# Transposes of the normalised block ahead of the attention output, the fold of the keys between the halves of the up-projection, and the gelu table load ahead of a copy

## The reference

```
x = x + xattn(layernorm(x), ctx)     # scores over 257 keys, 4 heads, top 32 kept, softmax, mean over heads,
                                     # @V; film; S4D convolution along 32 tokens; film; + residual;
                                     # h = gelu(layernorm(xt) @ W1 + b1) @ W2 + b2 (hidden 1024); layernorm
x = x + attn(layernorm(x))           # q, k, v; softmax(q k^T / 4) v, transposed and reshaped, @ wo^T
x = x + ffn(layernorm(x))            # 8 experts of hidden 128, top-2 gates (cosine + linear scores),
                                     # out = sum_e gate_e * (gelu(x @ w1_e + b1_e) @ w2_e + b2_e)
```

## Time and profile before

| | us |
|---|---|
| median of the runs | 654.56 |
| profiled execution | 650.08 |
| its span, first to last instruction | 648.1 |
| TensorE busy | 563.0 (87%) |
| VectorE busy | 519.7 (80%) |
| ScalarE busy | 304.0 (47%) |
| GpSimd busy | 270.8 (42%) |

### The profile page before, as it was taken

How to read it: one execution, slowest core, us unless ns; L and a number is a source line. 1 busy time by engine, 2 the same in 40 slices (tenths; PEclk the granted TensorE clock), 3 DMA queues, 4 the chain that set the end, 5 groups by cost and what they waited for, 6 DMA issues and landing times.

```text
span 648.1 us, 12648 instructions
## 1 busy us (share of the span) xinstructions
PE 563.0 (87%) x4314; PEld 420.1 (65%) x4314; DVE 519.7 (80%) x1772; ACT 304.0 (47%) x777; POOL 270.8 (42%) x629
## 2 busy tenths in 40 slices
PE   0148379778999999999999999999999999989967
PEld 0134234647787878787878787868687878776746
DVE  5599983686898989898989898989898989885443
ACT  5324001333646464646464646464646464635432
POOL 2742420235354545453535353535353636252421
PEclk9998565797999999999999999999999999999998
DMA  5196133030303030303030303030303030000000
GB/s 191 52 284 174 65 139 112 2 112 2 105 8 115 10 113 10 112 14 110 16 106 18 105 18 105 18 105 18 105 18 105 18 105 10 2 9 2 9 1 16
DMA packets 21127, 42.70 MB, mean 66 GB/s; under 512 B 5221, under 2 KB 13878, under 8 KB 20552
## 3 DMA queue, kind: packets, MB, share of 16 engines
q1 hardware_dynamic: 21064, 41.91, 20.6%
HBM read 39.73 MB, written 2.16 MB: 65 GB/s over the span
## 4 chain that ended last, share of the span: by engine, by line
PE 71%; DVE 4%; issue 3%; ACT 2%; POOL 2%; POOLq 0%; DVEq 0%
PE BB L1052 9%; PE D L1052 9%; PE BB L1075 8%; PE D L1069 7%; PE SS L1044 4%; PE SS L1045 4%; PE PC L1171 2%; PE PC L1206 2%; PE PC L1173 2%; PE BB L1129 2%; PE BB L1130 2%; PE BB L1166 2%; PE BB L1165 2%; PE SS L1027 2%; PE PC L1114 2%
## 5 line engine op out<-in xcount | busy, mean ns | idle before, releaser
L475 POOL TENSOR_SCALAR var_in<-mv 128x1 f32<-128x1 f32 x64 | 14.1, 220 | 249.9 <-DVE mv L780 143.8
L819 DVE MATCH_REPLACE8 work<-top,work 128x257 f32<-128x257 f32 x192 | 77.2, 409 | 0.0
L1052 PE MATMUL D<-ang,e_w 128*128 128x128 f32 x512 | 72.1, 288 | 0.0
L813 DVE MAX8 top<-work 128x8 f32<-128x257 f32 x192 | 70.9, 411 | 0.0
L1052 PEld LDWEIGHTS D<-ang,e_w 128*128 128x128 f32 x512 | 64.1, 198 | 10.1 <-issue 10.1
L1069 PE MATMUL D<-expw,ang 128*128 128x256 f32 x256 | 64.7, 383 | 1.2 <-ACT ang L549 0.9
L1052 PE MATMUL BB<-ang,w 128*128 128x128 f32 x512 | 64.6, 287 | 0.9 <-ACT ang L544 0.9
L1052 PEld LDWEIGHTS BB<-ang,w 128*128 128x128 f32 x512 | 61.5, 200 | 4.1 <-issue 2.7
L1075 PE MATMUL BB<-expw,ang 128*128 128x256 f32 x256 | 57.9, 379 | 0.0
L574 ACT ACTIVATE expo<-SS,nmax,srs 128x257 f32<-128x257 f32 x64 | 32.7, 562 | 46.4 <-DVE work L799 46.2
L1044 PE MATMUL SS<-ctx_t,qk 128*128 128x257 f32 x128 | 44.0, 428 | 10.8 <-DMA ctx_l<-in_ctx_l 5.0
(11 more groups left out here) (254 smaller groups left out, 1273.1 us busy)
## 6 DMA issues: line engine op xcount, KB each, us to landing
ctx_n<-in_ctx_n SPq DMA_DIRECT2D x16, 768.0 KB
ctx_t<-in_ctxT SPq DMA_DIRECT2D x16, 514.0 KB
ctx_t<-in_ctxT SPq DMA_DIRECT2D x16, 257.0 KB
x_all<-in_x SPq DMA_DIRECT2D x4, 512.0 KB, 5.4
xT<-in_xT SPq DMA_DIRECT2D x16, 128.0 KB, 2.3
out<-out_sb SPq DMA_DIRECT2D x16, 128.0 KB, 1.7
ctx_l<-in_ctx_l SPq DMA_DIRECT2D x64, 24.0 KB
w<-in_W SPq DMA_DIRECT2D x1, 1024.0 KB
```

The lines of the kernel that those rows point to most:

```text
L813: V.max(top[:, 2 * q + k, 8 * r8:8 * r8 + 8], work[:, 2 * q + k, :]).then_inc(chains["top"], 1)
L819: V.match_replace(work[:, 2 * q + k, :], top[:, 2 * q + k, 8 * r8:8 * r8 + 8], work[:, 2 * q + k, :], TAKEN).then_inc(chains["taken"], 1)
L1052: ins = MM(bank[:, 128 * m:128 * m + 128], w[:, k, at:at + 128], xs[:, 128 * k:128 * k + 128], start=k == 0, stop=k == 1)
```

## The change

The order of instructions changes on three engines. TensorE transposes hn before the output product instead of behind it, and does the first half of the up-projection before the fold, so that the fold stands between the halves. ScalarE runs the one-column gelu, and with it the table load, before the copy of the r product instead of behind it, and the first half's gelus before the fold's copies. VectorE makes hn before the last match-replaces of the first two sequences (`take8(a, 0, 3)`) instead of behind them. No instruction is added or removed.

```diff
@@ scalar engine, step
                 if following:
                     query(following)
+                if b:
+                    A(ahead[:, :], b1[:, 0:1], ACT.Gelu)
                 if c:
                     wait(act, s["r_mm"], one(c))
                     A(r_c[:, :, :, :].rearrange("p j b t -> p b j t"), C0[:, D:2 * D].rearrange("p (b j t) -> p b j t", b=BT, j=2), ACT.Copy).then_inc(s["r_a"], 1)
                 if b:
-                    A(ahead[:, :], b1[:, 0:1], ACT.Gelu)
                     wait(act, s["hT_mm"], one(b))
                     copy(hT[:, :], B0[:, 0:D], "hT_a")
+                if b:
+                    gelus(act1, 0, B1, b1, "w1a_mm", "ga_a", b)
                 if following:
                     keyed(following)
                 if b:
-                    gelus(act1, 0, B1, b1, "w1a_mm", "ga_a", b)
                     gelus(act1, 1, B0, b1, "w1b_mm", "gb_a", b)
@@ vector engine, step
                 if dd:
                     gated(range(4, 6))
-                if a:
-                    take8(a, 0, 3)
                 if b:
                     wait(dve, s["rs0_g"], one(b))
                     V.tensor_scalar(hn[:, :], xt[:, :], mv[0][:, 0:1], rstd[0][:, 0:1], ALU.subtract, ALU.mult).then_inc(s["hn_v"], 1)
+                if a:
+                    take8(a, 0, 3)
@@ tensor engine, step
                 if dd:
                     experts(range(8, NE + 1))
+                if b:
+                    wait(pe, s["hn_v"], one(b))
+                    wait(pe, s["xt_v"], one(b))
+                    transposes(B0, hn, "hT_mm")
                 if c:
                     wait(pe, s["r_a"], one(c))
...
                     ins.then_inc(s["o2_mm"], 1)
                 if b:
-                    wait(pe, s["hn_v"], one(b))
-                    wait(pe, s["xt_v"], one(b))
-                    transposes(B0, hn, "hT_mm")
+                    wait(pe, s["hT_a"], one(b))
+                    wide(0, B1, w1, hT, "w1a_mm")
                 if following:
                     if c:
                         wait(pe, s["x2_v"], one(c))
                     keyed(following)
                 if b:
-                    wait(pe, s["hT_a"], one(b))
-                    wide(0, B1, w1, hT, "w1a_mm")
                     wide(1, B0, w1, hT, "w1b_mm")
```

## The result

The changed kernel takes 649.16 us in the median (643.92 to 651.52, 14 runs) against 654.34 us (652.55 to 655.85, 14 runs) for the kernel before. The ratio is 0.9922, with a 95% interval of 0.9900 to 0.9943: 5.2 us less, where 4.6 were forecast. The profiled execution after took 645.32 us (span 643.3), the one before 650.08, so the traces explain 4.8 us.

What follows compares the result with a forecast made beforehand. TensorE was taken to bound the kernel, 71% of the span. Terms 4.4 - 0.7 + 0.5 - 0.2 + 0.6 = 4.6 us, off the 654.56 us median: 650.0 us, 8-in-10 range 647.2 to 652.6.

Steps and rivals of the forecast that it cites:

- The wait for x2: Step end on TensorE: the fold waits for VectorE's residual add x2; 0.47 us lost per step, to come back.
- The switch, 0.10 us: Entering the fold's 32-row tiles from whole-array products, now unhidden: 0.10 us per step, between none and 0.29.
- The step, 0.37 us forecast: Steps 3 to 14 on TensorE: 0.47 won less 0.10 for the switch, 4.4 us over twelve steps.
- ScalarE's margins: Cover on ScalarE: 0.3 us for hT, 0.5 before the r copy, 0.35 for the second gelus; nothing charged.
- VectorE's 0.21 us: x2 comes 0.21 us later behind the moved transposes; VectorE catches up at once, its second maximum having waited 0.44 us.
- Step 1, -0.7 forecast: No output product covers hT: 0.54 us lost plus a switch of about 0.2 at half clock.
- Step 2, +0.5 forecast: No experts: transposes fit into TensorE's wait for r; 0.72 us less the switch won.
- Step 15, -0.2 forecast; step 16, +0.6: Output product covers hT's wait, 0.64 us each; step 15 loses it again to later GpSimd weights for L1099.
- that the switch is free: Rival: the weight load's whole wait counts, 0.53 us per step, and switching costs nothing: 647.8 us, 13%.
- That ScalarE or VectorE eats half: Rival: late second gelus or late L1099 weights add 0.2 us of waiting per step: 652.4 us, 14%.
- That the table load fails to help: Rival: hT still late, first half waits 0.6 us per step, gain gone: 654.5 us, 4%.
- That the switch costs more than the wait: Rival: switching into the fold costs over 0.47 us per steady step; at 0.8 us, 659.7 us, 6%.

Runs made afterwards that it cites:

- without the split: Changed kernel with only the transposes moved ahead of the output product, the fold again in front of both up-projection halves: 32.354 us a steady step, 649.59 us.
- the two-part fold: Changed kernel with the fold in two pieces, the second after the first quarter of the up-projection's second half: 31.965 us a steady step, 649.88 us.
- The three undone edits: Changed kernel with one move taken back each: table load late 32.506, fold's copies before first gelus 32.78, hn late 32.817 us a steady step.
- the moved addition: GpSimd's addition of b2 put ahead of the normalisation's small operations: 639.7 us in the changed kernel, 645.5 us in the kernel before.

## Why the prediction was right, point by point

The forecast was 650.0 us, in a range of 647.2 to 652.6; measured were 649.16.

- **The wait for x2 comes back.** Right: the fold no longer waits for x2 in any step. The step without the split shows the wait again (0.5 us in 13 steps), so the split is what removes it.
- **The switch, 0.10 us.** Right: 0.10 to enter and 0.20 for a pair, by the two-part fold. The page TensorEngine Tiling (Array Packing), section Key Properties, of the Trainium skill says that a change of tiling mode drains TensorE; the runs agree in kind and give the price. The prediction's estimate of 0.17 us, from the Trainium skill's page TensorE: Matmul & The Clock Gate, section Single matmul latency, was too high by 0.07; that figure is stated for a bf16 product.
- **The step, 0.37 us forecast, 0.40 measured.** The term that was off is the output product to what follows: I took 0.90 us "as now", it was 0.86 (373.76 to 374.62). The reading behind it was incomplete: the prediction says that the output product starts where it does because the gate product is just done, but its weight load also waited 0.17 us for the copy of r, and its second pass started 0.25 us behind the first instead of 0.22. Twelve steps: 4.8 us instead of 4.4.
- **ScalarE's margins.** Forecast 0.3 us for hT (measured 374.34 to 374.62, 0.28), 0.5 us in front of the r copy (0.55), 0.35 us for the second gelus (0.60). The three undone edits show that each is needed: 0.47, 0.33 and 0.41 us of waiting.
- **VectorE's 0.21 us.** It is caught up at once, as forecast: the maximum's 0.44 us of waiting are gone and L1101 does not wait in steady steps.
- **Step 1, -0.7 forecast.** It lost 1.1 us (11.33 against 10.20). Mechanism right (the first half waits 0.47 us for hT), size off by 0.4. The clock was low there: the first half of the up-projection took 3.71 us in the profile after, the second 1.89, and how much of the step runs low was left open. In the profile after, 5.7 us of it were at half clock, before 4.3. The changed kernel with the moved addition, the same in step 1, had 4.6 us at half clock and took 10.94: 0.7 us more than before, as forecast.
- **Step 2, +0.5 forecast.** It won 3.4 us, and most of that is not the change: before, TensorE ran at granted clock 0.50 from 152 to 156 us; after, 150 to 156 is at 1.00 (windows above). Of the first eight experiments five have such a stretch there and three have none, in no order that the edits explain. The order's own part can be read where step 2 ran at full clock throughout: 30.16 us in TensorE's old order (the moves on ScalarE and VectorE alone), 29.58 in the new one, and 29.86 against 29.26 with the moved addition. So the change is worth 0.6 us there, as forecast, and the other 2.8 are luck of the execution. Step 16 had the opposite luck (below).
- **Step 15, -0.2 forecast; step 16, +0.6.** Step 15 won 0.75 us, as the covered wait for hT says, and L1101 waited 1.50 us (forecast about 1.4); by the count of the table that wait lies in step 16, so only the sum of the two terms, +0.4, can be compared. The loss came from what followed: a half-clock stretch that made step 16 1.8 us longer. The forecast had no such term. An execution with the same wait and full clock (the one without the split: 1.50 us, clock 1.00) has a step 16 of 31.29 us, so about 1.6 us of it is the clock. Without it the two steps win 0.5 us.
- **The ends together.** Forecast +0.2 us, and the profile has 0.0. That so little is off is partly luck: 2.8 us won by the clock in step 2 stand against 1.6 lost in step 16, 0.4 in step 1 and the unexplained 1.05 ahead of it. An estimate of the order's own part from the figures above is 4.8 - 0.7 + 0.6 + 0.5 = 5.2 us.
- **The median.** Taking the gain off the median assumed that the profiled execution's 4.5 us of distance would stay. It did, nearly: 3.8 us after. What it consists of was not asked; that it stayed nearly the same is luck in part, and its cause is not shown.

The rivals: that the switch is free falls (0.10 us). That ScalarE or VectorE eats half falls (no new wait in steady steps). That the table load fails to help falls too: its cover held, and undone it lengthens the step to 32.506 us, more than the whole gain. That the switch costs more than the wait falls.

## What to carry to other kernels

Two waits in a row on the engine that sets the pace can each be hidden behind the other's work, and moving only one of them makes the kernel slower: lay out the starts of all the neighbours before moving one. A switch between whole-array and 32-row products costs 0.1 us each way on TensorE, so an interleaving that removes a wait of 0.5 us pays and one that removes 0.1 us does not. When a small VectorE operation has two lengths in kernels that leave it alone, look for a GpSimd operation that starts beside it, and move that apart. Compare a run with the kernel before that was run beside it: here that kernel's median moved between 650.2 and 654.3 us.

## What the runs showed of the hardware

- A VectorE scaling of 128x32 takes 0.24 us or 0.82 us, the same in steps 3 to 14 of a profiled execution, when a GpSimd addition of 128x256 (0.72 to 0.77 us) starts about 0.06 us behind it. The Trainium skill, page SBUF — State Buffer, section Terms, says that the two engines share a port pair, which one of them holds for a whole instruction while the other is blocked. The trace agrees (the 0.82 us end 0.04 us after the addition), and shows beside it how a blocked instruction is recorded: one that takes 0.24 us when free stands there for 0.82, starts ahead of the addition and ends behind it. Held scalings have the addition 45 to 59 ns behind them, free ones 60 to 70 ns; whether that difference is the cause or a sign, no run tells.
- VectorE's block copy next to the scaling (pT_blk) takes 0.45 us where the scaling is free beside the addition, and 0.29 where the scaling is held or the addition is moved away.
- After waits of 1.42 to 1.50 us at the same place of step 16 the granted clock fell to half (2.4 to 1.2 GHz) for a few us in three kernels (step 16 of 32.85 to 32.91 us) and stayed at full in three others (30.93 to 31.29 us). What tells the two groups apart stays open.
